# Two PSUM banks per maximum instruction, and the value products in five groups per phase

## What is computed

```python
q = apply_rope((x @ Wq).reshape(B, T, 2 * H, HD), cos, sin)       # H = 16, HD = 4, T = 512
k = apply_rope((x @ Wk).reshape(B, T, 2 * KVH, HD), cos, sin)     # KVH = 8, repeated twice
attn1 = causal_attn(q1, k1, vcat, scale)                          # softmax over the keys up to the row
attn2 = causal_attn(q2, k2, vcat, scale)
attn = attn1 - lambda_full * attn2
attn = attn / sqrt(mean(attn * attn) + EPS) * rms_w * (1.0 - LAMBDA_INIT)
x = layernorm(x + attn @ Wo)
x = layernorm(x + moe(x))                                         # top-1 expert: silu(a) * g @ w2
```

## Time and profile before

| | us |
|---|---|
| median of 3 runs | 680.28 |
| lowest, highest | 674.95, 680.87 |
| the profiled execution | 670.18 |
| its span in the profile | 667.7 |

### The profile page before, as it was taken

One profiled execution on the slowest core, in us unless ns is written; L12 is line 12 of the kernel. 1 busy time (PEld: TensorE's weight loads), 2 busy tenths in 40 slices (PEclk: granted clock), 3 DMA queues, 4 the chain that ended last, 5 costly groups with the idle time before them and its releaser, 6 DMA issues.

```text
span 667.7 us, 19245 instructions
## 1 busy us (share of the span) xinstructions
PE 593.7 (89%) x6968; PEld 330.2 (49%) x6968; DVE 539.6 (81%) x1318; ACT 433.3 (65%) x903; POOL 415.3 (62%) x618
## 2 busy tenths in 40 slices
PE   3389899999989999998999999999988896999990
PEld 1134344344434444443444444343445785999990
DVE  6488988998998998899899889999746975666661
ACT  1105788887978887797888779787875343444441
POOL 6245257566877676687777668336363367687774
PEclk9576999999999999999999999999979996999995
DMA  3867566555664756666465655634129446465530
GB/s 112 262 211 246 159 197 217 165 177 183 186 197 123 231 162 190 202 183 194 113 229 167 213 190 166 192 115 117 46 60 329 138 137 189 136 196 189 196 125 24
DMA packets 70677, 114.54 MB, mean 172 GB/s; under 512 B 20028, under 2 KB 43068, under 8 KB 70300
## 3 DMA queue, kind: packets, MB, share of 16 engines
q1 hardware_dynamic: 58152, 76.22, 37.5%
q0 software_dynamic: 9168, 34.25, 14.9%
q10 hardware_dynamic: 3264, 2.85, 1.3%
HBM read 69.60 MB, written 47.27 MB: 175 GB/s over the span
## 4 chain that ended last, share of the span: by engine, by line
PE 53%; DVE 26%; DMA 6%; issue 6%; ACT 3%; POOL 2%; SPq 1%; ACTq 0%; POOLq 0%; DVEq 0%
DVE mr L1393 15%; PE bank L712 11%; PE bank L840 11%; PE bank L852 4%; PE bank L624 4%; PE bank L642 4%; PE bank L633 3%; DMA rows<-qk_parts 3%; PE bank L720 2%; PE bank L749 2%; PE bank L660 2%; PE bank L669 2%; PE bank L723 2%; ACT work L910 1%; PE bank L759 1%
## 5 line engine op out<-in xcount | busy, mean ns | idle before, releaser
L1393 DVE TENSOR_REDUCE mr<-bank 128x8 f32<-128x512 f32 x576 | 369.2, 681 | 43.7 <-PE bank L642 26.8
L910 ACT ACTIVATE work<-bank 128x512 f32<-128x512 f32 x576 | 313.5, 602 | 72.5 <-PE bank L669 51.4
L712 PE MATMUL bank<-work,v_aug 128*32 128x512 f32 (+7 forms) x2048 | 170.9, 418 | 0.0
L642 PE MATMUL bank<-rows 64*128 64x384 bf16 (+7 forms) x512 | 144.1, 292 | 0.0
L633 PE MATMUL bank<-rows 64*128 64x128 bf16 (+7 forms) x512 | 140.9, 293 | 0.0
L669 PE MATMUL bank<-qd,kz 64*128 64x384 bf16 (+7 forms) x512 | 137.0, 286 | 0.0
L660 PE MATMUL bank<-qd,kz 64*128 64x128 bf16 (+7 forms) x512 | 133.8, 287 | 0.0
L624 PE MATMUL bank<-bits 64*128 64x128 bf16 x448 | 100.8, 227 | 9.6 <-DVE mr L1393 8.6
L624 PEld LDWEIGHTS bank<-bits 64*128 64x128 bf16 x448 | 41.8, 94 | 121.5 <-DVE mr L1393 107.3
L651 PE MATMUL bank<-bits 64*128 64x128 bf16 x448 | 97.3, 224 | 0.0
L840 PE MATMUL bank<-xr,rows 128*128 128x256 f32 x368 | 86.6, 390 | 5.2 <-DVE xr L1619 4.6
(11 more groups left out here) (177 smaller groups left out, 1006.1 us busy)
## 6 DMA issues: line engine op xcount, KB each, us to landing
qk_apart<-apart SPq DMA_DIRECT2D x54, 256.0 KB, 3.6
rows<-qk_apart SPq DMA_DIRECT2D x64, 192.0 KB
kz<-qk_apart SPq DMA_DIRECT2D x64, 192.0 KB
qk_parts<-parts SPq DMA_DIRECT2D x90, 128.0 KB, 2.9
qk_apart<-apart POOLq DMA_DIRECT2D x42, 256.0 KB, 3.9
rows<-qk_parts SPq DMA_DIRECT2D x64, 96.0 KB
qd<-qk_parts SPq DMA_DIRECT2D x64, 96.0 KB
x_sorted<-in_c_pad SPq DMA_DIRECT2D x9, 390.0 KB, 4.3
```

The lines of the kernel that those rows point to most:

```text
L642: pe.matmul(bk[:, wa:T], qz[lo:lo + L, kv, i - 1].rearrange("p j l -> p (j l)"), kd[lo:lo + L, kv, 0:T - wa], start=False, stop=True, skip ...
L712: m = pe.matmul(pv_b[32 * t:32 * t + 32, L * kb:T], v_aug[:, vb, kv + v, kb, :], cols, start=kb == 0, stop=True, skip_group_check=True)
L910: nc.scalar.activation(prob[:, pos, r, :], st_b[no % ST_RING][:, :], ACT.Exp, scale=HD ** -0.5).then_inc(s_sfree, 1)
L1393: V.tensor_reduce(mr[:, s % 2, u % 2, i, i:i + NB], nat_b[no % NAT_RING][:, :].rearrange("p (n t) -> p n t", t=L), AX.X, ALU.max)\
```

## The change

1. `row_max` takes a slot t in place of a bank u: one `tensor_reduce` over both banks of the slot (128 x 1024 to 128 x 16). There are 288 of them in place of 576.
2. `nat_b` becomes two pairs of adjacent banks, each [128, 2, 512]. TensorE waits for a pair once per slot, at its first bank, and each bank's last matmul still counts up `s_nat`; readers wait for `NAT_IN`, the count of matmul groups, while releases are counted by `NAT_OUT`. A `FOR_DVE` user takes a whole pair and writes its first bank.
3. The ring for ScalarE, `st_b`, has three banks where it had four.
4. The steps of the products are issued in five slots in place of seven: 0 in slot 3 (512 columns), 1 and 2 in slot 5 (512), 3 and 4 in slot 7 (512), 5 and 6 in slot 0 of the next phase (512), 7 in slot 1 (256).
5. VectorE's small jobs of both u of a slot come behind the slot's one maximum and its `take`.

The diff, with renamings and waits that only follow from the above cut out:

```diff
-PV_AT = {3: [0], 5: [1], 6: [2], 7: [3], 8: [4]}
-PV_TAIL_AT = {0: [5], 1: [6, 7]}
+PV_AT = {3: [0], 5: [1, 2], 7: [3, 4]}
+PV_TAIL_AT = {0: [5, 6], 1: [7]}
...
             if g < NS:
-                for u in (2 * t, 2 * t + 1):
-                    nat["max", g, u] = len(nat_at)
-                    nat_out += 1
-                    nat_at.append(nat_out)
+                nat["max", g, t] = len(nat_at)
+                nat_in += 2
+                nat_out += 1
+                nat_filled.append(nat_in)
+                nat_at.append(nat_out)
...
                 if name in FOR_DVE:
                     nat[name, n] = len(nat_at)
+                    nat_in += 1
                     nat_out += 1
+                    nat_filled.append(nat_in)
                     nat_at.append(nat_out)
...
-NAT_NO, ST_NO, NAT_OUT, ST_OUT = rings()
-NAT_RING, ST_RING = 3, 4
+NAT_NO, ST_NO, NAT_IN, NAT_OUT, ST_OUT = rings()
+NAT_RING, ST_RING = 2, 3
...
-        banks = [bank(f"bank{i}") for i in range(8)]
-        nat_b, st_b, pv_b = banks[0:3], banks[3:7], banks[7]
+        nat_b = [ctx.enter_context(nc.psum_tensor(f"pair{i}", [P, 2, 512], F32)) for i in range(NAT_RING)]
+        st_b, pv_b = [bank(f"bank{i}") for i in range(ST_RING)], bank("products")
+        banks = [pair[:, r, :] for pair in nat_b for r in range(2)] + st_b + [pv_b]
...
-                return nat_b[NAT_NO["max", s, u] % NAT_RING]
+                return nat_b[NAT_NO["max", s, u // 2] % NAT_RING][:, u % 2, :]
...
-                    nat_wait(pe, NAT_NO["max", g, u])
+                    if u % 2 == 0:
+                        nat_wait(pe, NAT_NO["max", g, u // 2])
                     nat_mask(g, u)
...
-            def row_max(s, u):
-
-                no, i = NAT_NO["max", s, u], CH[u // 2]
-                if u < 2:
+            def row_max(s, t):
+
+                no, i = NAT_NO["max", s, t], CH[t]
+                if t == 0:
                     wait(dve, s_mt, 2 * (s - 1))
-                wait(dve, s_nat, no + 1)
-                V.tensor_reduce(mr[:, s % 2, u % 2, i, i:i + NB],
-                                nat_b[no % NAT_RING][:, :].rearrange("p (n t) -> p n t", t=L), AX.X, ALU.max)\
+                wait(dve, s_nat, NAT_IN[no])
+                V.tensor_reduce(mr[:, s % 2, :, i, i:i + NB],
+                                nat_b[no % NAT_RING][:, :, :].rearrange("p r (n t) -> p r n t", t=L), AX.X, ALU.max)\
                     .then_inc(s_nfree, 1)
...
             for g in range(PHASES):
-                for u in range(NU):
+                for t in range(NC):
                     if g < NS:
-                        row_max(g, u)
-                    if u % 2:
-                        for name, n in uses(g, u // 2):
-                            take(name, n)
-                    for name, b, k in jobs_at(g, u):
-                        job(name, b, k)
+                        row_max(g, t)
+                    for name, n in uses(g, t):
+                        take(name, n)
+                    for u in (2 * t, 2 * t + 1):
+                        for name, b, k in jobs_at(g, u):
+                            job(name, b, k)
```

## The result

| | before | changed |
|---|---|---|
| median of the runs | 678.52 us (674.95 to 680.87) | 692.57 us (686.87 to 693.50) |
| profiled execution | 670.18 us, span 667.7 | 692.27 us, span 690.4 |
| mean granted clock of TensorE | 0.952 | 0.947 |

The ratio is 1.0215, interval [1.0175, 1.0255]: the changed kernel is 2.1% slower, 14 us, where 5.5 us (0.8%) were forecast. The time is inside the range, on the side that the chances put second, and 6.6 us above the forecast. Measured as the working was made, profiled execution against profiled execution, it is further off: the spans differ by 22.7 us and 5.5 were forecast. The prediction carried the 10.1 us between before's profiled execution and its median over to the changed kernel, and that hid part of this: the changed kernel's profiled execution lies at its median, so nothing was to be carried.

The account below looks back on a forecast made before the run. TensorE bounds phase A, VectorE C and nearly B, neither D. +0.7 us per batch over 7.5 batches (+5.4), -1 in the first phases, +1 in the last, called +5.5 on 680.3: 686 us, range 669 to 696.

Parts of the forecast that it names:

- the 10.1 us carried over: Before's median of 680.28 us less its profiled 670.18, kept as a constant difference and added to the forecast profiled 675.7.
- the side that the chances put second: Slower than no change (above 687.1 us): chance 0.38, behind 0.44 for within and ahead of 0.18 for faster.
- A pair of banks costs 1.13: VectorE's maximum over two banks: pitch 1.13 us against 1.20 for two single ones, saving 0.07 for each of 288 pairs.
- Rival 2: VectorE's maxima: a pair costs what two cost, pitch 1.20 us, waits as computed; 694 us, chance 0.15.
- A +0.4: Phase with k, k2, wo: 16.2 us; k's wait 0.57, wo's pair 0.29, one way back 0.14 less.
- Rival 1: Slot 2: ScalarE frees its bank before TensorE asks, so the maxima's gain stays; 669 us, chance 0.22.
- Five groups save 0.14 in A: Products in phase A (k, k2, wo): removing groups saves TensorE one way back, 0.14 us per batch.
- B +0.4: Phase with v, turn_x1: 13.7 us; maxima 0.60 less, but VectorE waits 1.0 in slots 3 to 5.
- C -0.65: Phase with router, bounded by VectorE: 13.95 us; maxima save 9 x 0.067 = 0.60, and a small wait.
- D +0.6: Phase with rank, q, q2, turn_attn: 14.05 us; 0.79 at rank, a little at groups of slots 0, 3, 5, 7.
- The last two phases, +1: End of the attention stage, without maxima: ScalarE has one bank less, which costs 1 us.
- Rivals 2 and 3: Rival 3: missing ScalarE bank delays exponents, products and turn_ot in more slots, 0.3 us more per phase; 696 us, chance 0.10.

Follow-up runs that it names:

- singles_port: Kernel before with only guess's steps moved, to positions 4, 7, 8, 9 and 10 in place of 4 to 8: 706.33 us, ratio 0.9926.
- singles_4_3: Kernel before with four banks for VectorE and three for ScalarE, still one maximum per bank: 718.21 us, ratio 1.0098.
- 712 group: Set of eight follow-up runs beside which the kernel before had a median of 711 to 712 us; beside the first measurement it had 677 to 679.
- pairs_seven_groups: Changed kernel with the products in seven groups as before, in place of five: 712.58 us, ratio 1.0002 against the kernel before.

## Why the prediction was right and wrong

The time fell inside the range, and that is in part luck: three of the four phases were priced too low, the stage that repeats lost more than five times what was forecast, and the 10.1 us carried over covered part of it.

- **A pair of banks costs 1.13: right.** Records of 1.218 us (forecast 1.21), 1.13 to 1.14 from start to start (253.72 + 1.13 = 254.85, the next at 254.86). Rival 2 is gone.
- **A +0.4: right**, measured +0.42. k waits for ScalarE's exponent, and ScalarE's ring alone gives +0.55 less one way back. Rival 1 is gone with it. The first two phases took 1.03 less for 1 forecast, but that shows nothing: their end lies between 55.05 and 59.10 us in the traces, whatever the kernel.
- **Five groups save 0.14 in A: right**, 0.16.
- **B +0.4: wrong, +1.13.** The term is v's: in the stepping 0.59 us was given to its products and the way back, and rows of the kernel before show 0.99 (starts at 227.65, next mask at 228.64). ScalarE's copies of v were put at 1.3 and are 1.65. The prediction had the sign of it in hand: its stepping gave 13.3 us for this phase of before, and the rows have 13.61. With a ring of three, both lengths go straight into VectorE's wait, as k's do in A. The lines below, TensorE's timeline of before, were there to be read:

```profile
227.65 1.06 PE L730 MATMUL bank<-wv_s,xt_s 128*128 128x64 f32 x8
...
228.64 0.23 PE L624 MATMUL bank<-bits 64*128 64x128 bf16 x1
```

- **C -0.65: wrong, +0.33.** The step "9 x 0.067 = 0.60 and a small wait; here the change does what it says" took VectorE's busy 14.56 of 14.61 as work. 0.77 of it was a hold that ends with GpSimd's copy, and some 0.5 more the hold at the end of the phase; time saved ahead of the first is given back in it (0.51). The rest is the 0.47 of small steps that now touch. singles_port confirms the holds; the 0.47 is read from rows only.
- **D +0.6: right in its mechanism** (0.79 at rank; 0.76 more in the phase when the clock holds), **wrong in what follows**: TensorE's pauses of 1.8 us in all take its clock to 1.2 GHz for some 3 us, 1.45 us more. The stepping had TensorE at one speed throughout.
- **The third phase, +2.8, was not thought of,** and nothing ties it to the change. TensorE's clock is still rising there, 0.78 against 0.88, and the phase ends at 69.73 us in before and 71.51 in changed; but in the other traces it ends anywhere from 69.33 (singles_4_3) to 74.43 (singles_port), with pairs and without. So some 1.8 of the 22.7 us are a difference between two executions.
- **The last two phases, +1, did not come**: what lies behind the maxima took 0.22 less.
- **Rivals 2 and 3** had totals (694 and 696) nearer to the measured 692.6 than the forecast's 686, for reasons that did not apply: a pair does not cost what two banks cost, and ScalarE's ring did not take 0.3 us from every phase (nothing in C); one slot was priced too low.
- **The 10.1 us carried** from before's profiled execution to its median did not come. The profiled execution was forecast at 675.7 and took 692.27, 16.6 more; the median, with the 10.1 added, was forecast only 6.6 too low. Two errors stood against each other; that the median came out near is luck.

Per full batch with rank: forecast +0.75 and measured, with before's late load left out, +4.1. Of the 3.35 us between, 0.7 is v, 1.0 is C's two effects, 1.45 the clock, and 0.15 the rest of D.

What stays open: why the clock falls in three D phases of five in one execution and in all five of another; what the touching steps cost by themselves; why the kernel before's other executions take 5 to 11 us more than the profiled one; the pauses of the 712 group.

## What to carry to other kernels

Before an engine's busy time is called work, look for an instruction whose length depends on another engine: an addition of 0.95 us among ones of 0.18 was such a hold, and it swallowed what was saved ahead of it. Moving it by two places made the kernel 0.7% faster, where halving the number of maxima, with the banks that it took, made it 2.1% slower. Such a hold can turn on 0.05 us of arrival, so ask what an edit does to the meeting of the two engines. When instructions are merged, ask what each of them gave besides its result: here the small maxima stood between chained steps, and freed a bank every 0.6 us. And when a change makes TensorE wait where it never did, price the clock too, as half the speed for some microseconds.

## What the runs showed of the hardware

- VectorE reads two PSUM banks in one instruction, and the second bank costs its elements alone: 1024 fp32 elements per partition in 1.13 us from start to start against 0.60 for 512.
- A VectorE `tensor_scalar` on 64 fp32 columns in SBUF, issued while GpSimd copies bf16 in SBUF, ends 0.05 to 0.06 us after that copy does: 1.46 and 0.95 us in two kernels, 0.18 when issued behind the copies. Issued as a copy begins, it went through in 0.20 us in four batches of pairs_seven_groups, and the copy took 1.51 to 1.52 us in place of 1.47; in a fifth it was held for 1.51.
- A VectorE `tensor_tensor` on 8 bf16 columns, issued while GpSimd multiplies 512 fp32 columns in SBUF, ends 0.02 to 0.03 us after GpSimd does: 0.67, 0.69 and 0.88 us in three kernels, 0.16 to 0.20 where it meets a short GpSimd instruction.
- Two small VectorE instructions of which the second needs the first start 0.22 us apart, two that are independent 0.10. The Trainium skill ("VectorE: DVE Perf Modes", section "The DRAIN you can't avoid") says that a semaphore between two operations costs nothing extra; it measured long copies, and for instructions of 0.18 us these rows differ from it.
- Three pauses of TensorE of 0.45, 0.50 and 0.84 us within 3 us were followed by some 3 us at the 1.2 GHz level, in some phases and not in others of the same program.
- The same kernel ran at 677 to 679 us in some sets of runs and at 711 to 712 in others, 5% apart. The variants profiled there have phases equal to 0.02 us (A and C) up to the first D phase with rank, and in it stretches of 0.4 us and more in which TensorE, VectorE and ScalarE all stand. The record does not tie this to the chip.
